# Layer 2 of a four-layer graph network: 128 of 784 gathered edge columns come from TensorE, in batches of four, with a 16-bit one-hot matrix

## The reference, cut to what matters

```python
def _L2_gnn_ref(feats, Wq, bq, Wk, bk, Wv, bv, Wo, bo, Wf, bf, gamma, beta, src, dst):
    q = (feats @ Wq + bq).reshape(n, H, D)          # n = 3125, H = 4, D = 16
    k = (feats @ Wk + bk).reshape(n, H, D)
    v = (feats @ Wv + bv).reshape(n, H, D)
    score = jnp.sum(k[src] * q[dst], axis=-1)
    score = jnp.exp(jnp.clip(score / SCALE, -5.0, 5.0))
    wv = jax.ops.segment_sum(v[src] * score[..., None], dst, num_segments=n)
    z = jax.ops.segment_sum(score, dst, num_segments=n)
    wv = wv / (z[..., None] + 1.0)
    ...
```

## Time and profile before

| | us |
|---|---|
| device time, median of 3 runs | 6179.44 |
| lowest and highest of these | 6165.42, 6182.65 |
| span of the profiled execution, first to last instruction | 5335.3 |
| edge stage of layer 2, from its first DMA issue (3093.22) to its last store issue (4048.50) | 955.3 |
| VectorE busy over the span | 3848.7 (72%) |
| POOL busy | 3702.3 (69%) |
| PE busy | 3329.0 (62%) |

### The profile page before, as it was taken

The page is one execution under the profiler, slowest core; times in us unless marked ns, Lnnn a source line. Parts: engine busy times, 40 slices in busy tenths (PEclk is TensorE's granted clock), DMA queues, the critical chain, the costliest instruction groups (busy, mean ns, idle before and its releaser), DMA issues. The chain is left out here.

```text
span 5335.3 us, 59849 instructions
## 1 busy us (share of the span) xinstructions
PE 3329.0 (62%) x17449; PEld 2791.6 (52%) x17449; DVE 3848.7 (72%) x5210; ACT 2006.2 (38%) x3469; POOL 3702.3 (69%) x3472
## 2 busy tenths in 40 slices
PE   1777777753999999999999467777674700000001
PEld 0444444432888889988888467666673500000001
DVE  3888888874999999999999569999996522222223
ACT  0666666641344444444444223333332311111111
POOL 4777777764788888888887356766774077777774
PEclk8899999986999999999999679999996955555555
DMA  7777777764888888888887333333332922222221
GB/s 292 247 267 255 262 264 263 257 214 146 309 319 319 319 321 321 320 320 321 320 321 282 89 92 110 108 108 108 109 108 64 382 52 55 53 54 53 54 56 43
DMA packets 390718, 1060.91 MB, mean 199 GB/s; under 512 B 138843, under 2 KB 161943, under 8 KB 349241
## 3 DMA queue, kind: packets, MB, share of 16 engines
q1 hardware_dynamic: 229430, 755.21, 37.7%
q0 software_dynamic: 104704, 161.21, 12.0%
q10 hardware_dynamic: 56448, 142.93, 7.1%
HBM read 667.35 MB, written 391.75 MB: 199 GB/s over the span
## 5 line engine op out<-in xcount | busy, mean ns | idle before, releaser
L1458 PE MATMUL COLS<-CF,XF 128*128 128x256 f32 x6272 | 1485.4, 380 | 5.6 <-DVE XF L1566 5.6
L1458 PEld LDWEIGHTS COLS<-CF,XF 128*128 128x128 f32 x6272 | 1134.6, 190 | 129.3 <-DVE XF L1566 6.0
L909 ACT ACTIVATE OUT<-SC 128x576 f32<-128x576 f32 (+3 forms) x392 | 574.9, 1467 | 1346.3 <-DVE SC L846 989.8
L784 POOL DMA_INDIRECT G<-rel_tab,IDX_rel x784 | 739.6, 943 | 390.5 <-issue 249.1
L1425 POOL DMA_INDIRECT G<-x_tab,SRC x784 | 833.2, 1063 | 231.5 <-issue 219.2
L784 POOL DMA_INDIRECT G<-xl_tab,IDX_src x784 | 749.7, 956 | 275.0 <-issue 264.4
L784 POOL DMA_INDIRECT G<-kv_tab,IDX_src x686 | 647.1, 943 | 298.3 <-issue 221.6
L1785 PE MATMUL CP<-IDENT,LROW 128*68 128x128 f32 (+1 forms) x12 | 3.4, 422 | 1049.9 <-DVE SM L1906 1049.9
L838 DVE TENSOR_TENSOR MSG<-G,EW 128x512 f32<-128x512 f32 x98 | 100.0, 1020 | 733.3 <-DMA G<-rel_tab,IDX_rel 724.7
L1785 PEld LDWEIGHTS CP<-IDENT,LROW 128*68 128x68 f32 (+1 forms) x12 | 1.5, 157 | 1051.3 <-DVE SM L1906 1051.2
L1196 PE MATMUL PICK<-KV,HOT 125*128 125x128 f32 x2548 | 364.3, 309 | 204.6 <-ACT G L1215 202.5
(11 more groups left out here) (274 smaller groups left out, 6907.6 us busy)
## 6 DMA issues: line engine op xcount, KB each, us to landing
SHB<-ea9t SPq DMA_DIRECT2D x196, 1024.0 KB
wkv_tab<-WKV SPq DMA_DIRECT2D x98, 1024.0 KB
WKV<-wkv_tab SPq DMA_DIRECT2D x98, 1024.0 KB, 5.9
scan<-OUT ACTq DMA_DIRECT2D x196, 288.0 KB
scan<-OUT ACTq DMA_DIRECT2D x98, 576.0 KB
rel_tab<-YS SPq DMA_DIRECT2D x25, 2048.0 KB, 7.3
RAW<-spread SPq DMA_DIRECT2D x196, 256.0 KB
spread_q<-ZQ SPq DMA_DIRECT2D x98, 512.0 KB, 5.3
```

Source lines behind the costliest of these rows:

```text
L784: pool.indirect_dma_start(out=self.G[g][b][:, c, :], out_offset=None, in_=tab, in_offset=bass.IndirectOffsetOnAxis(ap=self.IDX[which][b][: ...
L909: nc.scalar.activation(self.OUT[b][:, :, 0:WD], SC[b][:, 0:WD, 1:1 + C].rearrange("p r j -> p j r"), ACT.Copy).then_inc(self.copied_out, 1)
L1458: nc.tensor.matmul(acc, XF[b][:, k, edges_], CF[:, k, :], start=(k == 0), stop=False)
```

## The change

The picked columns are no longer one in each chunk. From chunk 2 on the chunks take 1, 1 and 2 picked columns in turn, so that 128 columns are picked in 32 batches of four, and POOL gathers the other 656 (686 before). What it does, step by step:

- `project` also makes, for layer 2, KV3: the table TAB[:, :, 0:128] as three bfloat16 pieces (high on ACT; the rest REST on VectorE; middle on ACT before the second WHI; low on VectorE before the third WLO), and NODE16, the node numbers as 16-bit integers, each written 128 times along the row (VectorE). Both stay in SBUF, so `edges_2` no longer loads KV.
- SyncE loads SRC, all source numbers, once, and POOL reads its indices there; the load of IDX_src for each chunk is gone. For each batch SyncE loads the 512 source numbers of its four columns, spread over all partitions by the transfer (SRC4), and ACT narrows them to 16 bits (ID16).
- VectorE compares ID16 with NODE16 into HOT (bfloat16), one compare of 125x3200 elements for each picked column: four for a batch, for the batch two ahead, two in the first step of a batch and one in the other two. The first compare of a step stands behind `scores`, the second behind `sums`. Both inputs lie in SBUF.
- TensorE forms PICK the other way round: 3 x 25 products with a piece of the table as the weights and 512 columns of HOT as the moving side. ACT takes PICK into TURNED, TensorE turns its four blocks back (BACK), and ACT places one or two of them in G.
- VectorE and POOL have all 98 steps written out.

```diff
+PICK_FROM = 2
+BATCHES = (NCH - PICK_FROM) // 3
+def picks(t):
+    return 0 if t < PICK_FROM else 2 if (t - PICK_FROM) % 3 == 2 else 1
...
+                        if pieces is not None:
+                            act.wait_ge(m_copied, len(units))
+                            nc.scalar.activation(KV3[:, :, 0, :], TAB[:, :, 0:128], ACT.Copy).then_inc(kv_high, 1)
...
+                            nc.vector.tensor_copy(NODE16[:, :, :], NODE[:, :].unsqueeze(2).to_broadcast([P, K, P]))\
+                              .then_inc(numbered, 1)
+                            v.wait_ge(kv_high, 1)
+                            nc.vector.tensor_tensor(REST[:, :, :], TAB[:, :, 0:128], KV3[:, :, 0, :], ALU.subtract)\
+                              .then_inc(kv_rest, 1)
...
-                e = Edges(ctx, 2, [(kv_tab, 128, "src")], {"src": src_ap})
+                e = Edges(ctx, 2, [(kv_tab, 128, "src")], {})
...
+                        def load_sources(i):
+                            wait(sp, narrowed, i - 1)
+                            sp.dma_start(SRC4[i % 2][:, :], src4_ap[i:i + 1, :].to_broadcast([P, 4 * P]))\
+                              .then_inc(src4_in[i % 2], 16)
...
+                            wait(pool, e.scanned, t - 1)
+                            for c in range(C - picks(t)):
+                                pool.indirect_dma_start(
+                                    out=e.G[0][b][:, c, :], out_offset=None, in_=kv_tab,
+                                    in_offset=bass.IndirectOffsetOnAxis(ap=SRC[:, t * C + c:t * C + c + 1], axis=0),
+                                ).then_inc(e.rows_in[0][b], 16)
...
+                        for i in range(BATCHES):
+                            wait(pe, compared, 4 * i + 4)
+                            wait(pe, taken, i)
+                            for piece in range(3):
+                                for k in range(K):
+                                    ins = nc.tensor.matmul(PICK[:, :], KV3[N, k, piece, :], HOT[i % 2][N, k, :],
+                                                           start=(piece == 0 and k == 0), stop=(piece == 2 and k == K - 1))
+                            ins.then_inc(picked, 1)
+                            wait(pe, taken, i + 1)
+                            wait(pe, placed, 3 * i)
+                            for q in range(4):
+                                ins = nc.tensor.transpose(BACK[:, q * P:(q + 1) * P], TURNED[:, q * P:(q + 1) * P],
+                                                          IDENT[:, :])
+                            ins.then_inc(turned_back, 1)
...
+                        def compare(i, q):
+                            wait(v, narrowed, i + 1)
+                            wait(v, picked, i - 1)
+                            nc.vector.tensor_tensor(HOT[i % 2][N, :, q * P:(q + 1) * P],
+                                                    ID16[i % 2][N, q * P:(q + 1) * P].unsqueeze(1).to_broadcast([NP, K, P]),
+                                                    NODE16[N, :, :], ALU.is_equal).then_inc(compared, 1)
...
-                            nc.vector.tensor_tensor(HOT[N, ks, :], SPREAD[N, 0:P].unsqueeze(1).to_broadcast([NP, m, P]),
-                                                    NODE_F[N, ks].unsqueeze(2).to_broadcast([NP, m, P]), ALU.is_equal)\
...
+                            if t < PICK_FROM:
+                                ahead = [(1, 2 * t), (1, 2 * t + 1)]
+                            else:
+                                i, r = divmod(t - PICK_FROM, 3)
+                                ahead = [(i + 2, q) for q in ((0, 1), (2,), (3,))[r] if i + 2 < BATCHES]
                             e.expand(v, t, n, b, first)
...
                             scores(t, n, b, first)
...
+                            if ahead:
+                                compare(*ahead[0])
                             e.sums(v, t, n, b, first, e.G[0][b][:, :, 64:128])
...
+                            if ahead[1:]:
+                                compare(*ahead[1])
+                        all_chunks(step)
```

More of the change, by code:

```diff
@@ L352, in _, with project @@
                     nc.tensor.transpose(PR[1][0:64, 0:64], wcol("comp"), IDENT[0:64, 0:64]).then_inc(tposed, 1)
[L357 removed]
+        def project(weights, n_out, biases, tables, keep, spread_at=None, spread_tab=spread, width=64, relations=None, pieces=None):
             per = 512 // n_out
@@ L781, in step @@
                     pool.sem_inc(parked, 1)
-                    for c in range(self.gathered):
+                    for c in range(C):
                         for g, (tab, _, which) in enumerate(self.tables):
@@ L1208, in _, with narrow, take @@
                     @block.scalar
                     def _(act):
+                        def narrow(i):
+                            wait(act, src4_in[i % 2], (i // 2 + 1) * 16)
+                            wait(act, compared, 4 * (i - 1))
+                            nc.scalar.activation(ID16[i % 2][:, :], SRC4[i % 2][:, :], ACT.Copy).then_inc(narrowed, 1)
+                        def take(i):
+                            wait(act, picked, i + 1)
+                            wait(act, turned_back, i)
+                            nc.scalar.activation(TURNED[:, :], PICK[:, :], ACT.Copy).then_inc(taken, 1)
@@ L1210, in _ @@
+                        narrow(0)
+                        narrow(1)
                         wait(act, e.ready, e.N_READY)
-                        def place(t, b):
-                            wait(act, picked, t + 1)
-                            wait(act, e.scanned, t - 1)
-                            nc.scalar.activation(e.G[0][b][:, C - 1, :], PICK[:, 0:128], ACT.Copy).then_inc(placed, 1)
                         def step(t, n, b, first, last):
@@ L1255, in scores @@
+                        e.constants(nc.vector)
+                        for q in range(4):
+                            compare(0, q)
+                        wait(v, e.ready, e.N_READY)
                         def scores(t, n, b, first):
                             st = Steps(v, e.a_steps, t * 2)
-                            wait(v, e.rows_in[0][b], (n + 1) * (16 * e.gathered))
-                            wait(v, placed, t + 1)
+                            wait(v, e.rows_in[0][b], ROWS_AT[t] * 16)
+                            if picks(t):
+                                wait(v, placed, t - PICK_FROM + 1)
```

131 lines of the change are left out of this document (60 added, 71 removed).

## The result

The changed kernel takes 5934.65 us (median of 4 runs, 5926.17 to 5951.66), the kernel before beside it 6172.43: ratio 0.962, 95% interval 0.960 to 0.964. It is faster; the forecast was 6226 us, slower, and its range began at 6155.

The account below looks back on a forecast made before the run. VectorE was taken to set layer 2's pace with POOL close behind, POOL becoming the bound after the change. Fewer gathers and `project` (-112 us) plus stalls (+159) gave +47 on 6179: 6226 us, range 6155 to 6275.

Parts of the forecast that it names:

- the sum: Whole kernel: -112 + 159 = +47 us on the profiled span, the 844 us outside the trace staying; forecast 6226 us.
- Gathers without the rest: Layer 2's gathers on POOL: 656 at layer 3's rate of 1.261 us take 826 us instead of 942, minus 116 us.
- `project`: Stage before layer 2's edges: making NODE16 and the table's pieces delays the first gather by 4.5 us, bounds 0 and 14.
- The compare: VectorE in layer 2: a 16-bit compare of 3200 elements runs at two elements a cycle, 1.83 us.
- Rival C: VectorE in layer 2: compares run at one element a cycle, 3.49 us each; +255 us, 6434 us; chance 0.08.
- That it stops gathers: POOL in layer 2: compares with two SBUF inputs stop gathers; stall is length - offset - 0.13; 159 us for 128 compares.
- Rival B: POOL in layer 2: 16-bit compares don't stop gathers, so no stalls; 6077 us; chance 0.12.
- The offsets: Layer 2 batches: first compares begin 0.13 to 0.35 us ahead of the fourth gather, stalling 1.5 us; the second compare 0.6.
- the turning point: Layer 2's stalls: below a mean of 0.88 us per compare (112 / 128) the change gains.
- Rival A2: Layer 2: compares fall just behind a gather's start, stalling 0.6 us instead of 1.5; -7 us, 6172 us; chance 0.18.
- A: Main case for layer 2: compares just ahead of a gather stall it 1.5 us; 6226 us, range 6199 to 6265; chance 0.60.
- The scan: POOL's wait for SC of two chunks back in layer 2: adds nothing after the change.

Follow-up runs that it names:

- 16 bits once: The kernel before with HOT and the table once in bfloat16, lower bits left out: 6133.03 us, ratio 0.981 with pauses; 5329.3 us, 0.9987 without.
- One piece: The changed kernel with one of the table's three pieces, 25 products a batch instead of 75: 5850.28 us, ratio 0.947 with pauses; 5320.39 us, 0.9972 without.
- looped: The changed kernel with TensorE's 32 batches in a loop instead of written out: 6014.81 us, ratio 0.962 with pauses; 5322.27 us, 0.9972 without.
- the kernel with TensorE idle: The kernel before with all columns of layer 2 gathered by POOL, without compares, products or placing: 6074.26 us, ratio 0.972 with pauses; 5379.16 us, 1.008 without.

## Why the prediction was wrong

**The step that failed** is the one in the sum: "the 844 us between it and the median of 6179.44 lie outside the trace and stay". They lay inside, in pauses that the profiled execution didn't have. Where the pauses were traced, 316 us of them were in layer 2 (1258 - 942); the changed kernel has 106 there (1031 - 925) or, on another chip, 89 (1014 - 925), so 210 to 227 less, against a measured gain of 238. The prediction had named "a change outside the span" as what could make it wrong and gave it no chance.

**What the pauses of layer 2 follow** is shown in part. Two edits take products from TensorE and leave the gathers, the compares' length and the hand-overs as they are. (The counts are mine, from the records; one with the f32 one-hot has two.)

- 16 bits once has 2,646 products where the kernel before has 5,096, and loses 212 us where that loses 316 (1149 - 937, 1258 - 942; two pausing chips): 42 ns a product.
- One piece has 928 where the changed kernel has 2,528, and loses 11 us instead of 89 (936 - 925, 1014 - 925; one pausing chip): 49 ns a product. TensorE's busy time falls with the number in both (664 to 352 us, 610 to 265, without pauses), so these runs don't tell the two apart.

The change itself takes 2,568 products away: 75 products of 512 columns for four picked columns take the place of 200 passes of 128, 208 with the spreading. At 42 ns that is 108 us, an estimate, and so about half of the 210 to 227. The rest needs another cause: 16 bits once has nearly the number of the changed kernel, with less busy time, and still loses 212 us where the changed kernel loses 89 to 127 (127 looped: 1052 - 925); on the one chip where both ran it took 6133 us and the looped form 6015. The two differ in VectorE, busy for 889 of 944 us in one and 762 of 930 in the other (without pauses), and in how often the picked columns are handed over, in each chunk or once in three. No run separates these.

The 98 us of the kernel with TensorE idle are no floor below the others: VectorE's late instructions, 406 there, don't occur in the layer of the kernel before (0 of 1,150), and one piece loses 11 us. And the price holds for layer 2 alone: layer 0 loses 424 us with 2,514 products, layer 1 36 with 8,437, layer 3 83 with none. Why instructions come late on these chips stays open.

**Within the trace**, against the comparison without pauses (5336 to 5319, -17 us, where +47 was forecast):

- *Gathers without the rest*, -116: measured 925.3 - 107 of stalls = 818, so -124. The rate is 818 / 655 = 1.249 us and not 1.261, since the pause between two gathers is 0.31 us here and 0.32 in layer 3.
- *`project`*, +4.5: the first gather starts at 3100.7 instead of 3097.4, +3.3. Right.
- *The compare*, 1.83 us: 1.82. Rival C is out.
- *That it stops gathers*: right, and so is the rule with its 0.13, also for 16 bits. Rival B is out, and the removal of the second tile input took every stall away. The Trainium skill's rule on two SBUF inputs (SBUF — State Buffer, Who interferes with whom) agrees with both; its inference that a tensor_tensor leaves descriptor making alone doesn't: 2.09 us against 0.94.
- *The offsets*: this term was mis-sized. One place, 0.13 to 0.35 us ahead of the fourth gather, was worked out for all three steps of a batch; the steps differ. The compare follows T after 1.54 us in each, where 1.63 was said. In the first step T comes 2.91 us after the gather (3388.34 to 3391.25) and the compare stands 0.54 us ahead of the fourth gather. In the second T comes at 3.08, but the last gather is itself the one that the second compare stopped, 1.49 us long, so the next ones start later and the compare is 0.93 ahead. In the third T comes at 2.60 (3407.02 to 3409.62) and the compare is 0.87 ahead. The stalls are 1.15, 0.80 and 0.83 us instead of 1.5 each. The second compare was forecast at 0.6 and gives 0.54. Sum 107 instead of 159 us, 0.84 per compare. The prediction had put the turning point at 0.88: the change lands just on the winning side.
- *Rival A2* comes nearest by its number (-7 us, a mean stall below 0.9), but by luck: it has rows land 0.3 us later and the compare behind the start of a gather, where in the first and third step they land 0.1 to 0.6 earlier, and the compare stands further ahead of it.
- *The range*: its lower end for A, 6199, doesn't follow from its two reasons (30 x 3 x 0.15 = 13.5 and 4.5 us from 6226 give 6208), and the 1.87 us of its upper end is more than the whole compare of 1.83.
- *The batch*: 28.3 us instead of 30. *TensorE*: 580.6 / 32 = 18.1 us of busy time for a batch, forecast 19; without pauses nobody waited for it. *The scan*: without pauses POOL has no row of waiting for SC. Both right. With pauses neither holds: 11 waits, 107.7 us.

With these sizes the sum is -124 + 3 + 107 = -14, and the last gather moved from 4039.4 to 4026.0, -13.4.

## What to carry to other kernels

Compare the profiled execution's span with the times before anything else: here 14% between them was no launch cost but time inside the layers, and it changed with the kernel; a forecast is then needed for each kind of execution. TensorE's instructions cost time in layer 2 though its busy time was hidden: on a pausing chip fewer products won (the layer took 1014 us with three pieces and 936 with one) even where the trace at hand shows nobody waiting for them. And take the lag from a gather to its reader for each step of a repeating pattern, with the stalls that the change itself brings: the offset decides how much of a two-tile compare a gather feels. Or give VectorE one tile and a scalar.

## What the runs showed of the hardware that was not expected

- Six chips, two kinds: the kernel before took 5336 to 5340 us on three and 6182 to 6255 on three. The granted clock of TensorE in the changed kernel was 0.81 without pauses and 0.78 with them.
- With pauses, gaps come in steps of about 0.70 us: TensorE's 1.74, 2.43 and 3.13 above. With TensorE idle, 406 of the 861 register and semaphore instructions of VectorE during the gathers took 0.6 to 0.8 us; without pauses none did, and their medians by kind were 0.02 to 0.06. The transfers take the same time in both: the median packet of the gathers' queue takes 81 ns over the whole kernel before.
- The trace of a pausing execution holds fewer semaphore changes: about 5,700 in layer 2 of the kernel before, against 17,400 without pauses, for the same program. So "issue" and "remote" in its rows can stand for a wait that the trace lost; the readings of TensorE above rest on gaps where the program has no wait, and the prices on spans. Whether the lost changes and the late instructions have one cause was not tried.
- 800 compares of 125x512 16-bit elements with a scalar took a median of 344 ns, and no gather beside them took more than 1.002 us.
